# Second attention: 32 array rows per head for the transposed scores only

## The chip, the cores and the metric

One core of one Trainium2 chip runs the kernel. The time is device microseconds of one execution; three runs of the kernel before gave 1461.8, 1468.85 and 1471.88 us, and their median, 1468.85 us, is the time before.

## The reference

Two transformer layers on 2048 tokens of width 128, in float32, each modulated by vectors of a conditioning input. The first has a spectral attention (a real FFT of chunks of 64 tokens, attention on the four lowest frequencies, a causal convolution on the others) and a gated feed-forward of width 512. The second has plain attention and a mixture of eight experts, of which the two best are used. The change lies in the attention of the second layer. The core of what it must compute:

```python
qkv = (jnp.einsum('bnd,ed->bne', x, qkv_w) + qkv_b).reshape(b, n, H, 3 * HD)   # H = 16, HD = 8, n = 2048
q, k, v = jnp.split(qkv, 3, axis=-1)
...
attn = jax.nn.softmax(jnp.einsum('bhqd,bhkd->bhqk', q, k) * SCALE, axis=-1)
out = jnp.einsum('bhqk,bhkd->bhqd', attn, v)
```

## The kernel before

Five engine programs are written out by hand, and semaphores alone set the order between them. On TensorE the program is one list: what is written first runs first.

**Heads in strips.** The 16 heads form four groups (hg) of four heads (g). Head g of a group owns the 32 partitions 32g to 32g + 31. Of these, 24 hold the eight numbers of q or k three times, as parts of a split into a coarse and a fine half, so that one matmul in the reduced float format (F32R) gives products of almost full precision. Partitions 24 and 25 of the strip carry the negated maximum of each query on the side of the queries, and ones on the side of the keys. Ks holds the keys and Qs the queries of all 2048 tokens in this layout, Qp a padded copy of 512 queries: for each head a full 128-partition tile in which only that head's strip is not zero. GpSimd zeroes Qp once (L306) and refills the strips for each block of queries (L315). With all 128 rows in a matmul, the zeros of Qp keep the other three heads out of the sum.

**Two kinds of scores.** Natural scores (nat, L778) have queries on the output's partitions and serve only to find each query's maximum over the keys: 128 queries of one head against 2048 keys, four matmuls of 512 keys into PSUM banks 0 to 3. VectorE reduces two banks at a time (maxima, L1221). Transposed scores (L841) have keys on the partitions: one key tile of 128 keys (kt) against 512 queries of one head, with the maximum already subtracted by the two extra rows, into banks 4, 5 and 7 in turn (score_bank). ScalarE takes their exp into probs (L495). The values (L817) multiply probs by V; head g writes the 16 partitions from 32g of bank 6, and each is a full-precision matmul that the hardware does in two passes.

**The steps.** There are four blocks of 512 queries (qb), four groups, 16 key tiles: 256 steps (step, L821). A step s issues, in this order: L841 for heads 0 and 1; the last of the four natural matmuls of the item 20 steps ahead minus one (LEAD = 20); the four value matmuls of the step before (L808); L841 for heads 2 and 3; the first three natural matmuls of the item 20 steps ahead. The last 20 steps have no natural scores left to do. At key tile 2 four transposes of the outputs of the group before are added (turn_outputs, L805), at key tile 13 four transposes of the maxima of the next group (max_rows, L791). The chain of waits counts a step from L841 of heads 2 and 3.

**The waits.** L841 needs its bank free, that is the exp of two or three scores earlier (L835). L778 needs the maxima of its two banks (L777). L817 needs the exps of its step (L815). The first L841 of a group waits until the maxima of the group are in Qp (L825): VectorE copies them out of PSUM (L1245) and SyncE sends them in eight transfers (L277).

**Neighbouring work of other shapes.** Three other matmuls use few array rows: the mask of the first attention (L618, 32 rows, bf16, directly before L620 with 128), and two small ones of the experts (L949 and L961, 8 rows).

Of the kernel before, what the change touches and what calls it, by code (L numbers as in the profile page):

```python
# [19 lines left out]
P = 128  # L20
# [49 lines left out]
def adaln_pair(nc, x_in, consts_in, mods_in, spectral_in, ffn_in, attn_in, moe_in, out):  # L70
    with ExitStack() as ctx:
        def sb(name, shape, dt=F32, where=ctx):
            return where.enter_context(nc.sbuf_tensor(name, shape, dt))
# [78 lines left out]
        with l1:  # L152
            Ks = sb("Ks", [P, HG, TOK], F32R, where=l1)
            Qs = sb("Qs", [P, HG, TOK], F32R, where=l1)
            Qp = sb("Qp", [P, HG, G4, 512], F32R, where=l1)
# [47 lines left out]
        def bank(n):  # L203
            return ps[:, n, :]
# [8 lines left out]
        def due(count):  # L213

            return not isinstance(count, int) or count > 0
# [8 lines left out]
        score_bank, order = [], [4, 5, 7]  # L224
# [6 lines left out]
        def items_since(n):  # L231

            return next(d for d in range(1, 64) if score_bank[(n - d) % 64] == score_bank[n])
# [333 lines left out]
        def _(pe):  # L567
# [79 lines left out]
            for ri in range(2):  # L647
                pe.wait_ge(sem.gelu_ready, ri + 1)
                for half in range(2):
                    n = 2 * ri + half  # L650
# [115 lines left out]
            def nat(qb, k, c):  # L766

                hg, qt, g = k // 16 % 4, k % 16 // 4, k % 4
                item = 64 * qb + k
                if c == 0 and k % 16 == 0:  # L770
                    if isinstance(qb, int) and qb == 0 and k == 0:
                        pe.wait_ge(sem.first_filled, G4)
                    else:
                        pe.wait_ge(sem.qpad_filled, 4 * (4 * qb + k // 16))
                if c % 2 == 0:
                    if due(2 * item + c // 2 - 1):
                        pe.wait_ge(sem.nat_max, 2 * item + c // 2 - 1)  # L777
                mm = pe.matmul(bank(c), Qp[:, hg, g, qt * P:qt * P + P], Ks[:, hg, c * 512:c * 512 + 512],  # L778
                               start=True, stop=True)
                if c % 2:  # L780
                    mm.then_inc(sem.nat_ready, 1)

            def max_rows(qb, grp):

                pe.wait_ge(sem.m_step, 4 * (4 * qb + grp + 1))
                if due(4 * qb + grp):
                    pe.wait_ge(sem.o_norm, 4 * qb + grp)

                    pe.wait_ge(sem.exp_done, 256 * qb + 64 * (grp - 1) + last_in_bank_7(rows_kt) + 1)
                for qt in range(4):  # L790
                    last = pe.transpose(ps[0:8, 7, qt * P:qt * P + P], m2[:, qt, :], ident)  # L791
                last.then_inc(sem.mT_ready, 1)

            def turn_outputs(qb, grp):

                pe.wait_ge(sem.u_copied, 4 * qb + grp)
                pe.wait_ge(sem.o_norm, 4 * qb + grp)
                pe.wait_ge(sem.mT_copied, 4 * qb + grp + 1 if not (isinstance(qb, int) and 4 * qb + grp == 16) else 16)

                if isinstance(qb, int) and 4 * qb + grp == 16:  # L800
                    pe.wait_ge(sem.exp_done, 1024)
                else:
                    pe.wait_ge(sem.exp_done, 256 * qb + 64 * grp + last_in_bank_7(turn_kt) + 1)
                for qt in range(4):
                    last = pe.transpose(ps[:, 7, qt * P:qt * P + P], U[:, qt * P:qt * P + P], ident)  # L805
                last.then_inc(sem.uT_ready, 1)

            def values(qb, s):  # L808

                hg, kt = s // 16 % 4, s % 16  # L810
                if kt == 0:
                    if due(4 * qb + s // 16):
                        pe.wait_ge(sem.u_copied, 4 * qb + s // 16)
                for g in range(G4):
                    pe.wait_ge(sem.exp_done, 256 * qb + 4 * s + g + 1)  # L815
                    col = (4 * hg + g) * VW
                    last = pe.matmul(ps[32 * g:32 * g + VW, 6, :], V[:, kt, col:col + VW],  # L817
                                     probs[:, 4 * (s % 2) + g, :], start=(kt == 0), stop=(kt == 15))
                last.then_inc(sem.pv_ready, 1)

            def step(qb, s):  # L821
                hg, kt = s // 16 % 4, s % 16
                last_block = isinstance(qb, int) and qb == TB - 1
                if kt == 0:
                    pe.wait_ge(sem.mrow_in, 128 * (4 * qb + s // 16 + 1))  # L825
                for g in range(G4):

                    if g == 2 and not (isinstance(qb, int) and qb == 0 and s == 0):
                        if not (last_block and s - 1 + LEAD >= 64):
                            nat(qb, s - 1 + LEAD, 3)  # L830
                        values(qb, s - 1)
                    n = 4 * kt + g
                    free = 256 * qb + 4 * s + g - items_since(n) + 1
                    if due(free):
                        pe.wait_ge(sem.exp_done, free)  # L835
                    if n > 4 * turn_kt + 6 and n == min(m for m in range(4 * turn_kt + 7, 64) if score_bank[m] == 7):
                        pe.wait_ge(sem.o_norm, 4 * qb + s // 16 + 1)
                    if n > 4 * rows_kt + 6 and n == min(m for m in range(4 * rows_kt + 7, 64) if score_bank[m] == 7) \
                            and not (last_block and s // 16 == 3):
                        pe.wait_ge(sem.mT_copied, 4 * qb + s // 16 + 2)  # L840
                    pe.matmul(bank(score_bank[n]), Ks[:, hg, kt * P:kt * P + P], Qp[:, hg, g, :],  # L841
                              start=True, stop=True).then_inc(sem.st_ready, 1)
                if not (last_block and s + LEAD >= 64):
                    for c in range(3):
                        nat(qb, s + LEAD, c)
                if kt == turn_kt and not (isinstance(qb, int) and qb == 0 and s < 16):
                    turn_outputs(qb, s // 16)
                if kt == rows_kt and not (last_block and s // 16 == 3):
                    max_rows(qb, s // 16 + 1)
# [20 lines left out]
            for s in range(4):  # L870
                step(0, s)
            with pe.Fori(0, TB - 1) as qb:
                for s in range(4, 68):
                    step(qb, s)
            for s in range(4, 64):
                step(TB - 1, s)
# [605 lines left out]
```

## Time and profile before

| | |
|---|---|
| median of three runs | 1468.85 us (1461.8 to 1471.88) |
| profiled execution, span from first to last instruction | 1474.4 us |
| instructions | 19927 |
| mean granted TensorE clock | 0.960 |
| TensorE busy | 1334.6 us, 91% |
| TensorE weight loads busy | 798.2 us, 54% |
| VectorE busy | 879.9 us, 60% |
| ScalarE busy | 816.9 us, 55% |
| GpSimd busy | 52.3 us, 4% |

The span is the profiled execution's own time, and the only one given for it; the runs were timed apart from it. PE is a matmul, PEld a weight load; the two overlap. A matmul's duration goes from its start to the landing of its last result, so neighbours overlap too: the distance between two starts is what one costs. A matmul with many neighbours of its own shape is recorded with its weight load already done; where the load is not hidden, it is inside the recorded duration. Shapes are written rows*columns of the array.

### The profile page before, as it was taken

The page shows a single profiled execution, that of the slowest core. Times are in us where ns is not written, and L with a number is a line of the kernel's source. Part 1 is how long each engine was busy: PE and PEld are TensorE (multiplying, and loading weights), DVE is VectorE, ACT ScalarE, POOL GpSimd, SP SyncE. Part 2 cuts the span into 40 slices and gives each one's busy share as a digit, 9 for nine tenths or more (in the row PEclk, how much of TensorE's full clock was granted, in tenths as well). Part 3 has the DMA queues.
Part 4 walks back from the last instruction along what each step waited for, and adds up shares of the span by engine and source line. Part 5 has one row for each costly group of instructions (what it writes and reads, how often), then busy time and mean ns, then how long its engine had stood idle before and what let it go on. Part 6 is the DMA issues. An engine that isn't in the chain of part 4 may idle for free.

```text
span 1474.4 us, 19927 instructions
## 1 busy us (share of the span) xinstructions
PE 1334.6 (91%) x6846; PEld 798.2 (54%) x6846; DVE 879.9 (60%) x1244; ACT 816.9 (55%) x1426; POOL 52.3 (4%) x71
## 2 busy tenths in 40 slices
PE   5776999588999998999999999999999969999998
PEld 4434788334454453554444455445443337787877
DVE  4756442698877785787776777778774052222222
ACT  2425443342666675667665667667666754344342
POOL 0001000110000000000000000000000000000000
PEclk9867999899999999999998999999999989999999
DMA  8000000000000000000000000000000000000000
GB/s 334 1 1 0 0 0 1 0 0 1 1 1 2 1 1 3 2 1 1 2 2 2 2 2 1 1 2 1 1 2 1 1 0 1 8 1 8 0 7 7
DMA packets 9280, 14.83 MB, mean 10 GB/s; under 512 B 4320, under 2 KB 8544, under 8 KB 8672
## 3 DMA queue, kind: packets, MB, share of 16 engines
q1 hardware_dynamic: 8896, 10.84, 2.1%
q10 hardware_dynamic: 288, 2.76, 0.5%
q8 instruction: 53, 0.87, 0.3%
q14 instruction: 43, 0.35, 0.1%
HBM read 12.29 MB, written 1.05 MB: 9 GB/s over the span
## 4 chain that ended last, share of the span: by engine, by line
PE 75%; DVE 11%; ACT 5%; SPq 4%; DMA 3%; issue 2%; DVEq 0%; ACTq 0%
PE ps L841 18%; PE ps L817 15%; PE ps L778 13%; PE ps L941 8%; PE ps L687 5%; SPq L277 4%; PE ps L689 4%; PE ps L688 4%; DVE mx L1221 3%; DMA Qp<-mT 2%; ACT eh L547 2%; PE ps L724 1%; PE ps L922 1%; DMA x<-x_in 1%; ACT probs L495 1%
## 5 line engine op out<-in xcount | busy, mean ns | idle before, releaser
L1221 DVE TENSOR_REDUCE mx<-ps 128x1 f32<-128x1024 f32 x512 | 608.2, 1219 | 187.4 <-PE ps L778 185.4
L495 ACT ACTIVATE probs<-ps 128x512 f32<-128x512 f32 x1024 | 554.2, 595 | 277.7 <-PE ps L841 262.6
L841 PE MATMUL ps<-Qp,Ks 128*128 128x512 f32 x1024 | 356.9, 430 | 34.1 <-DMA Qp<-mT 23.1
L778 PE MATMUL ps<-Ks,Qp 128*128 128x512 f32 x1024 | 330.4, 404 | 15.4 <-DVE mx L1221 8.3
L841 PEld LDWEIGHTS ps<-Qp,Ks 128*128 128x128 f32 x1024 | 171.3, 191 | 290.0 <-ACT probs L495 226.2
L817 PE MATMUL ps<-probs,V 128*16 128x512 f32 x2048 | 275.5, 607 | 0.0
L778 PEld LDWEIGHTS ps<-Ks,Qp 128*128 128x128 f32 x1024 | 192.3, 191 | 85.8 <-DVE mx L1221 34.3
L547 ACT ACTIVATE eh<-ps,MW 128x512 f32<-128x512 f32 x128 | 88.0, 688 | 95.3 <-PE ps L689 94.6
L941 PEld LDWEIGHTS ps<-MW,eh 128*128 128x128 f32 x1024 | 118.3, 192 | 2.6
L941 PE MATMUL ps<-MW,eh 128*128 128x128 f32 x1024 | 119.2, 275 | 0.0
L1362 DVE SCALAR_TENSOR_TENSOR acc<-ps,gate,acc 128x128 f32<-128x128 f32 x128 | 36.0, 344 | 129.3 <-PE ps L941 128.8
L817 PEld LDWEIGHTS ps<-probs,V 128*16 128x16 f32 x2048 | 34.3, 94 | 91.4 <-ACT probs L495 65.3
L315 POOL CAST Qp<-Qs 32x512 fp32r (+1 forms) x60 | 36.6, 610 | 678.8 <-PE ps L841 648.8
L687 PE MATMUL ps<-hT,ew 128*128 (+1 forms) x128 | 56.7, 443 | 2.8
L689 PE MATMUL ps<-hT,ew 128*128 (+1 forms) x128 | 50.4, 394 | 0.0
L688 PE MATMUL ps<-hT,ew 128*128 (+1 forms) x128 | 50.4, 393 | 0.0
L1176 DVE TENSOR_TENSOR act_b<-bf,act_b 128x512 fp32r<-128x512 f32 x16 | 11.1, 692 | 58.9 <-ACT bf L442 58.9
L687 PEld LDWEIGHTS ps<-hT,ew 128*128 128x128 f32 x128 | 24.0, 188 | 26.7 <-ACT eh L547 21.6
L1252 DVE RECIPROCAL rden<-ps 128x16 f32<-128x16 f32 x16 | 4.0, 249 | 53.0 <-PE ps L805 53.0
L753 PE MATMUL ps<-hT,AW 128*128 128x512 f32 x64 | 32.7, 608 | 0.9 <-ACT hT L344 0.9
L677 PE MATMUL ps<-CW,z 128*128 128x128 f32 x48 | 11.7, 409 | 21.9 <-DVE z L993 21.9
L689 PEld LDWEIGHTS ps<-hT,ew 128*128 128x128 f32 x128 | 24.1, 188 | 5.7
(215 smaller groups left out, 1049.6 us busy)
## 6 DMA issues: line engine op xcount, KB each, us to landing
MW<-moe_in SPq DMA_DIRECT2D x1, 4454.0 KB, 23.7
FW<-ffn_in SPq DMA_DIRECT2D x1, 2824.5 KB, 12.4
Qp<-mT SPq DMA_DIRECT2D x128, 2.0 KB, 1.7
SW<-spectral_in ACTq DMA_DIRECT2D x1, 1479.5 KB, 9.8
DW<-mods_in ACTq DMA_DIRECT2D x1, 1219.0 KB, 6.4
x<-x_in SPq DMA_DIRECT2D x4, 256.0 KB, 10.8
out<-x SPq DMA_DIRECT2D x4, 256.0 KB, 2.3
AW<-attn_in SPq DMA_DIRECT2D x1, 836.5 KB, 13.7
```

Source lines behind the costliest of these rows:

```text
L277: sp.dma_start(Qp[row:row + 1, hg, g, :].bitcast(F32), mT[4 * part + g:4 * part + g + 1, :].bitcast(F32)) \
L315: pool.tensor_copy(Qp[rows, hg, g, :], Qs[rows, hg, cols(qb, 512)]) \
L495: act.activation(probs[:, 4 * (s % 2) + g, :], bank(score_bank[4 * (s % 16) + g]), ACT.Exp, scale=SCALE1) \
L547: act.activation(eh[:, e % 2, fb, :], bank(fb % 2), ACT.Relu, bias=mw["eb1"][:, col:col + 1]).then_inc(sem.eh_copied, 1)
L687: pe.matmul(to, w[0], v[0], start=start, stop=False)
L688: pe.matmul(to, w[0], v[1], start=False, stop=False)
L689: return pe.matmul(to, w[1], v[0], start=False, stop=stop)
L778: mm = pe.matmul(bank(c), Qp[:, hg, g, qt * P:qt * P + P], Ks[:, hg, c * 512:c * 512 + 512], start=True, stop=True)
L817: last = pe.matmul(ps[32 * g:32 * g + VW, 6, :], V[:, kt, col:col + VW], probs[:, 4 * (s % 2) + g, :], start=(kt == 0), stop=(kt == 15))
L841: pe.matmul(bank(score_bank[n]), Ks[:, hg, kt * P:kt * P + P], Qp[:, hg, g, :], start=True, stop=True).then_inc(sem.st_ready, 1)
L941: last = pe.matmul(ps[:, 2 + e % 2, qt * P:qt * P + P], eh[:, e % 2, fb, qt * P:qt * P + P], mw["ew2"][:, col:col + P], start=(fb == 0), s ...
L1221: dve.tensor_reduce(mx[:, k // 16 % 2, k % 16, pair:pair + 1], ps[:, 2 * pair:2 * pair + 2, :].rearrange("p b n -> p (b n)"), AX, ALU.max) \
```

## The change

In step, the transposed scores slice both operands to the 32 partitions of their head. The natural scores still use 128 partitions and the padded queries, and everything else is as before.

```diff
@@ -838,7 +838,8 @@
                     if n > 4 * rows_kt + 6 and n == min(m for m in range(4 * rows_kt + 7, 64) if score_bank[m] == 7) \
                             and not (last_block and s // 16 == 3):
                         pe.wait_ge(sem.mT_copied, 4 * qb + s // 16 + 2)
-                    pe.matmul(bank(score_bank[n]), Ks[:, hg, kt * P:kt * P + P], Qp[:, hg, g, :],
+                    rows = slice(32 * g, 32 * g + 32)
+                    pe.matmul(bank(score_bank[n]), Ks[rows, hg, kt * P:kt * P + P], Qp[rows, hg, g, :],
                               start=True, stop=True).then_inc(sem.st_ready, 1)
                 if not (last_block and s + LEAD >= 64):
                     for c in range(3):
```

## Rows read from the trace of the kernel before

**Rows 1.** The page: TensorE's busy time, and its granted clock in 40 slices.
```profile
PE 1334.6 (91%) x6846; PEld 798.2 (54%) x6846; DVE 879.9 (60%) x1244; ACT 816.9 (55%) x1426; POOL 52.3 (4%) x71
PEclk9867999899999999999998999999999989999999
```
**Rows 2.** Stretches of time: us, busy time of each engine, clock, DMA.
```profile
562.00:774.00 212.00, 202.08 (x1060) 102.33 (x1056) 158.38 (x157) 141.05 (x260) 9.76 (x16) 0.98 0.01 2
...
1127.00:1181.00 54.00, 47.70 (x239) 16.55 (x232) 1.23 (x3) 39.47 (x77) 0.00 (x0) 0.97 0.01 1
```
**Rows 3.** The page's costliest groups: busy us, mean ns of one, idle before.
```profile
L841 PE MATMUL ps<-Qp,Ks 128*128 128x512 f32 x1024 | 356.9, 430 | 34.1 <-DMA Qp<-mT 23.1
L778 PE MATMUL ps<-Ks,Qp 128*128 128x512 f32 x1024 | 330.4, 404 | 15.4 <-DVE mx L1221 8.3
...
L817 PE MATMUL ps<-probs,V 128*16 128x512 f32 x2048 | 275.5, 607 | 0.0
```
**Rows 4.** Chain of waits, one step: start us, us, what.
```profile
700.68 0.66 PE ps L841 x2
701.34 0.70 PE ps L778 x3
702.03 0.46 PE ps L841 x2
702.49 0.23 PE ps L778
702.72 0.98 PE ps L817 x8
```
**Rows 5.** Timeline, ScalarE and VectorE in that step: start, us, what [idle before].
```profile
701.14 2.24 ACT L495 ACTIVATE probs<-ps 128x512 f32<-128x512 f32 x4 [0.78 <-PE ps L841]
...
701.84 2.36 DVE L1221 TENSOR_REDUCE mx<-ps 128x1 f32<-128x1024 f32 x2 [0.66 <-PE ps L778]
```
**Rows 6.** Timeline of TensorE around L949, a matmul of 8 rows.
```profile
1224.73 0.39 PE L689 MATMUL ps<-hT,ew 128*128 128x512 f32 x1
1225.05 1.05 PE L949 MATMUL ps<-CW,scT 8*128 8x8 f32 x8
1226.04 0.50 PE L687 MATMUL ps<-hT,ew 128*128 128x512 f32 x1
```
**Rows 7.** Timeline of weight loads around L618, a matmul of 32 rows.
```profile
45.10 0.97 PEld L620 LDWEIGHTS ps<-Kp,QT 128*128 128x128 f32 x8 [0.23 <-issue]
46.19 0.09 PEld L618 LDWEIGHTS ps<-mcol,mrow 32*128 32x128 bf16 x1
46.51 0.30 PEld L620 LDWEIGHTS ps<-Kp,QT 128*128 128x128 f32 x2 [0.23 <-issue]
```
**Rows 8.** Timeline of loads and matmuls: a pair L841, and the first of L817.
```profile
700.61 0.30 PEld L841 LDWEIGHTS ps<-Qp,Ks 128*128 128x128 f32 x2 [0.85 <-ACT probs L495]
...
702.64 0.12 PEld L817 LDWEIGHTS ps<-probs,V 128*16 128x16 f32 x6 [0.35 <-ACT probs L495]
...
702.64 0.62 PE L817 MATMUL ps<-probs,V 128*16 128x512 f32 x4
```
**Rows 9.** Chain of waits in the last 20 steps.
```profile
1150.83 0.61 ACT probs L495
...
1151.47 0.49 PE ps L841
```
**Rows 10.** Timeline of TensorE around a group's end.
```profile
716.19 0.73 PE L841 MATMUL ps<-Qp,Ks 128*128 128x512 f32 x2
...
718.89 0.72 PE L841 MATMUL ps<-Qp,Ks 128*128 128x512 f32 x2 [1.27 <-DMA Qp<-mT]
...
720.76 0.73 PE L841 MATMUL ps<-Qp,Ks 128*128 128x512 f32 x2
```
**Rows 11.** Chain of waits ahead of that matmul, one issue and the last transfer.
```profile
713.28 0.59 SPq L277
...
717.07 1.70 DMA Qp<-mT
```

## The prediction

> **What bounds the kernel now.** First the page: TensorE is busy 91% of the span and its granted clock is 0.9 to 1.0 of full speed where the second attention runs [rows 1]. The stretches by time place that attention: about 355 to 1181 us, in four blocks of queries; over 562 to 774 us TensorE is busy 202 of 212 us, VectorE 158, ScalarE 141 [rows 2]. So TensorE sets the pace, if the others really wait for it. The groups say which work this is: 1024 transposed scores (L841), 1024 natural ones (L778), 2048 half passes of the values (L817), 963 us of matmul together [rows 3].
>
> Then one step (one key tile of four heads) in the chain of waits: two L841 take 0.66 us, three L778 0.70, two L841 0.46, one L778 0.23, eight L817 0.98, ending at 703.70, 3.02 us after the step's start [rows 4]. The chain never leaves TensorE. The other engines confirm it: ScalarE's four exps take 2.24 us and begin after 0.78 us of waiting for L841, VectorE's two maxima take 2.36 us after 0.66 us of waiting for L778 [rows 5]. A shorter TensorE step would shorten the kernel by up to about 0.6 us a step before VectorE binds; a longer one lengthens it at once.
>
> The reader should see one more thing: the same two matmuls cost 0.66 us behind L817 and 0.46 behind L778 [rows 4]. This 0.20 is what the rest turns on.
>
> **The change, part by part.** It adds and removes no instruction. L841 reads 32 rows of the array instead of 128. That has two effects.
>
> First, a change of array shape between neighbours. Matmuls of 128 rows, 128 columns and 512 elements follow each other by 0.23 us (three in 0.70 [rows 4]), and the next weights are loaded under the running one. L689 begins at 1224.73; the next, L949, has 8 rows, and begins 0.32 later; going back, L687 at 1226.04 lasts 0.50 instead of 0.39 to 0.40, because its weight load (0.11 us of array time) stands in the open [rows 6]. So one switch costs (0.32 - 0.23) + (0.50 - 0.39) = 0.20 us, the same as the difference in the chain. Is it the rows, or a semaphore? L618 (32 rows) to L620 (128 rows) has no wait between: L618's weights at 46.19, L620's at 46.51; and from L620 to L618, 46.19 follows on eight loads that ended at 46.07, instead of beginning under the last matmul [rows 7]. Both directions pay without a semaphore in play. I take 0.195 a switch; from these rows it can hardly be under 0.19 or over 0.20.
>
> A step has two switches today, L778 to L817 and L817 to L841. After the change it has five: L817 to L841 and L778 to L817 remain, and L841 to L778, L778 to L841, L841 to L778 are new. Three times 0.195 is 0.585 us a step.
>
> Second, the two L841 that stand side by side now lie in different strips of 32 rows and write different PSUM banks. No row here shows two row strips at work together, so their gain is bounded. One end is nothing: today's pairs take their 0.23 us each in turn. The other end is the nearest relative, L817, where four matmuls in four strips of columns, 0.60 us each, fit in 0.62 us, and their weight loads (six in 0.12 us) overlap too [rows 8]. By that a pair costs one matmul plus about 0.01, a gain of 0.22; two pairs give 0.44 a step. Between them: matmuls overlap but weight loads don't. The pair's loads take 0.30 us today [rows 8] and one has 0.11 of array time, so the second starts 0.11 behind the first, and a pair gains 0.12, two 0.24. I take 0.44, since L817 is the same array cut the other way.
> The Trainium skill states this directly ("TensorE: Matmul & The Clock Gate", Part 3, The mechanism: weight loads overlap only where row groups differ, and tiles start about 4 ns apart). By it the gain is the one that I took; no run here shows it for rows yet.
>
> A step so becomes 3.02 + 0.585 - 0.44 = 3.165 us, 0.145 longer.
>
> How many steps: L778's 1024 matmuls are 256 items, of which 20 are done ahead of the first step, so 236 steps have natural scores. The last 20 have none. There the chain goes L841, exp 0.61, L841 0.49, values, over and over [rows 9]: their switches exist already, and the two L841 around the exp can't be paired, because the second waits for the exp of the first. No gain, no loss.
>
> Where a stall gives back: at a group's end TensorE waits for the eight transfers of the maxima. The step that starts at 716.19 takes 4.57 us, 1.55 more than others, and the matmul waits 1.27 us for the DMA [rows 10]. From the copy of the maxima to the landing nothing depends on TensorE: eight issues of 0.59 us one after the other and 1.70 of transfer [rows 11]. Two steps run under it, so twice the lengthening is absorbed as long as that is under 1.5 us: 0.29 at each of the 14 group ends among the 236 steps. That is as if 28 of the steps cost nothing: 208 x 0.145 = 30 us.
>
> What I cost at nothing: VectorE and ScalarE do the same work with longer waits. The exp of the third head must end before the weights of the next step's second L841 can load; today that wait doesn't show: two L841 behind L778 keep their 0.46 [rows 4], and a new switch puts 0.2 us more ahead of that load. POOL's fill of the padded queries, the zeroed tile and the transfers stay as they are. If the cover failed, up to 0.2 us at a few steps would be exposed, some us in all.
>
> **Sum:** the profiled span is 1474.4 us; no device time of that execution stands beside it, and it lies 5.5 us over the median of the runs, 1468.85. The difference is added to the median: 1468.85 + 30 = 1499 us.
>
> **Rivals.**
> A. Weight loads of the two strips come one after the other: 0.585 - 0.24 = 0.345 a step, 0.69 absorbed at group ends, 208 x 0.345 = 72 us, 1541 us. For it: today's loads stand 0.11 apart. Against it: L817's overlap.
> B. No overlap at all between row strips: 0.585 a step, still under the 1.5 absorbed, 122 us, 1591 us. For it: no row shows it for rows. Against it: the columns do it.
> C. Faster. The place is the three new switches; the price that decides is 0.44 / 3 = 0.147 us. If the weight load across a switch were hidden for strips (a load into rows that the running matmul doesn't use) only 0.09 of each would remain: 3 x 0.09 - 0.44 = -0.17 a step, 208 x -0.17 = -35 us, 1434 us, with VectorE's 2.36 still inside a step of 2.85. Against it: L618 and L689 to L949 pay in full though one side has few rows.
> D. Nothing happens: the slice doesn't make the array smaller, or price and gain cancel within the measurement. The slices of 32 and 8 rows elsewhere do show as 32 and 8 rows with a switch [rows 6, 7], so only the cancelling is left: a switch of about 0.15 to 0.17.
> A fall of the granted clock is no case of its own: in the last 20 steps TensorE waits for ScalarE every step and was granted 0.97 [rows 2].
>
> **How the numbers follow.** My forecast has a chance of 0.60; its own range is 1489 to 1510 (switch 0.185 to 0.205, pair gain 0.21 to 0.23, some us for a stall that shifts). A 0.17, B 0.06, C 0.08, D 0.09. Below 1484 and above 1545 lie C, most of D and B, about 0.2 in all. A measurement tells 1% (15 us) from no change: slower 0.83, same 0.09, faster 0.08.
>
> **What would show it.** L841 with 32 rows; steps of about 3.17 us; in the chain, three L778 taking 0.89 instead of 0.70 and the single one 0.43; weight loads of a pair a few ns apart (A: 0.11 apart, B: matmuls 0.23 apart); each new weight load starting about 0.32 us after the start of the last matmul; group ends with a DMA wait of about 1.0 us. I am wrong if L778's weights load under L841 across the switch, if a pair doesn't overlap, or if the granted clock falls inside the blocks.

## The result: 6.5% slower, and the profile after

The changed kernel takes 1568.21 us (median of four runs, 1553.31 to 1581.53) against 1468.64 (the kernel before, a fourth run added): ratio 1.0648, 95% interval 1.0581 to 1.0715. Medians here are of all runs, ratios of each kernel's fast runs alone (here without the 1581.53). Forecast were 1499 us and a range up to 1545. The sign was right and the size was not: about 100 us instead of 30.

The steps themselves came out as forecast. The chain of waits of the changed kernel, one step at full clock (start us, us, what), answers to [rows 4]:

```profile
701.62 0.42 PE ps L842 x2
702.05 0.89 PE ps L778 x3
702.94 0.43 PE ps L842 x2
703.38 0.42 PE ps L778
703.80 0.98 PE ps L817 x8
704.78 0.43 PE ps L842 x2
```

L842 is the old L841. The step takes 3.16 us (704.78 - 701.62; forecast 3.165, before 3.02). A pair behind L817 costs 0.42 where it cost 0.66. Three L778 cost 0.89 where they cost 0.70, the single one 0.42 where it cost 0.23: the new switches. The timeline of the same step shows the overlap (PE is a matmul, PEld a weight load):

```profile
701.55 0.18 PEld L842 LDWEIGHTS ps<-Qp,Ks 32*128 32x128 f32 x2 [0.85 <-ACT probs L495]
...
701.55 0.49 PE L842 MATMUL ps<-Qp,Ks 32*128 32x512 f32 x2
```

The pair's loads take 0.18 us for both, against 0.30 in [rows 8], and its matmuls 0.49 for both: two row strips work side by side, as the four column strips of L817 do. The Trainium skill's figure for this ("TensorE: Matmul & The Clock Gate", Part 3, The mechanism: tiles start about 4 ns apart) is confirmed to the rounding of the rows.

Then the same chain 60 us earlier:

```profile
643.96 0.72 PE ps L842 x2
644.68 1.58 PE ps L778 x3
...
646.98 0.72 PE ps L778
647.70 1.84 PE ps L817 x8
649.54 0.72 PE ps L842
```

The same work, but 5.58 us (649.54 - 643.96). Every piece is stretched, and nothing waits for another engine. The stretches of time tell why (start and end, length, busy time of PE, PEld, DVE, ACT and POOL with the number of instructions, and behind POOL the granted clock):

```profile
531.00:553.00 22.00, 22.00 (x68) 8.20 (x68) 9.15 (x11) 8.95 (x17) 0.00 (x0) 0.50 0.00 1
...
597.00:655.00 58.00, 54.81 (x168) 18.52 (x164) 25.14 (x23) 22.31 (x41) 0.00 (x0) 0.56 0.01 2
...
915.00:1215.00 300.00, 293.71 (x1509) 110.64 (x1507) 222.86 (x222) 201.06 (x372) 7.29 (x12) 1.00 0.01 1
...
1229.00:1278.00 49.00, 40.40 (x171) 9.74 (x170) 0.55 (x2) 27.96 (x54) 0.00 (x0) 0.64 0.00 0
```

TensorE was granted 0.50, its level of 1.2 GHz ("half clock" below), for long stretches. The slices of the page show them against [rows 1]:

```profile
PE 1431.1 (91%) x6846; PEld 725.3 (46%) x6846; DVE 882.0 (56%) x1244; ACT 817.0 (52%) x1426; POOL 52.1 (3%) x71
PEclk9768998995999796599998889999999678999999
```

TensorE is 91% busy in both kernels, so the busy share says nothing here. The mean granted clock does: 0.906 against 0.960. With only two levels, a mean clock c over a span S means 2(1 - c)S at the lower one: 295 us against 118. The expectations below count half-clock time so. A good part of it is not the change's: in both kernels some 80 us lie ahead of the first step and 14 to 19 behind the last. Inside the steps the traces have 199 us against 24.

The account of the 97 us between the profiled spans (1571.5 and 1474.4), from the distances between one step's values (L817) and the next one's in both traces:

- The first step's values begin 2 us later.
- 198 of the first 235 distances ran at full clock in both kernels. Group ends included, they add 25 us.
- The other 37 ran at half clock at least in part, in one kernel or in both. They add 57 us.
- The last 20 steps add 14 us. Ten of them took 4.03 us or more, where most had taken 2.63.

Together 98 us; behind the steps half a microsecond comes back. The steps' own 0.147 us is also in the 37, some 5 us. So the price of the steps is 30 us, as forecast, and the clock's is about 67, most of it in some 24 steps at 5.58 instead of 3.17. In the last 20 steps the chain reads:

```profile
1225.19 1.84 PE ps L817 x8
1227.03 0.77 PE ps L842 x3
1227.80 0.60 ACT probs L495
1228.44 0.79 PE ps L842
1229.23 1.84 PE ps L817 x8
```

Here 128 rows had run at 0.97 of the full clock [rows 2, second row], also with a wait for an exp in each step.

### The profile page after: what moved, and what is told of

Its sections match the earlier page's. It is cut to its first block, busy times and chain, and to the rows that moved or that the text cites. A ratio compares the mean times of both kernels' runs of the same rounds, so it can differ in the third digit from the quotient of the medians.

```text
span 1571.5 us, 19927 instructions
## 1 busy us (share of the span) xinstructions
PE 1431.1 (91%) x6846; PEld 725.3 (46%) x6846; DVE 882.0 (56%) x1244; ACT 817.0 (52%) x1426; POOL 52.1 (3%) x71
## 4 chain that ended last, share of the span: by engine, by line
PE 76%; DVE 10%; ACT 5%; SPq 4%; DMA 2%; issue 2%; DVEq 0%; ACTq 0%
PE ps L778 19%; PE ps L817 16%; PE ps L842 14%; PE ps L942 7%; PE ps L687 5%; SPq L277 4%; PE ps L689 4%; PE ps L688 4%; DVE mx L1222 3%; DMA Qp<-mT 2%; ACT eh L547 1%; PE ps L724 1%; PE ps L923 1%; ACT probs L495 1%; DMA x<-x_in 1%
## 5 line engine op out<-in xcount | busy, mean ns | idle before, releaser
L778 PE MATMUL ps<-Ks,Qp 128*128 128x512 f32 x1024 | 407.7, 482 | 14.6 <-DVE mx L1222 7.4
L842 PE MATMUL ps<-Qp,Ks 32*128 32x512 f32 x1024 | 279.4, 537 | 36.2 <-DMA Qp<-mT 18.0
L817 PE MATMUL ps<-probs,V 128*16 128x512 f32 x2048 | 304.6, 668 | 0.0
L842 PEld LDWEIGHTS ps<-Qp,Ks 32*128 32x128 f32 x1024 | 104.1, 196 | 385.0 <-ACT probs L495 301.6
L778 PEld LDWEIGHTS ps<-Ks,Qp 128*128 128x128 f32 x1024 | 185.1, 203 | 178.2 <-issue 92.4
L817 PEld LDWEIGHTS ps<-probs,V 128*16 128x16 f32 x2048 | 34.6, 96 | 71.1 <-issue 55.7
L753 PE MATMUL ps<-hT,AW 128*128 128x512 f32 x64 | 32.7, 608 | 0.9 <-ACT hT L344 0.9
```

The lines of the kernel that those rows point to most:

```text
L842: pe.matmul(bank(score_bank[n]), Ks[rows, hg, kt * P:kt * P + P], Qp[rows, hg, g, :], start=True, stop=True).then_inc(sem.st_ready, 1)
```

## The experiments

Medians are in us; ratios are to the kernel before, with 95% intervals; two experiments have none. Half-clock times are those of the one profiled execution of each kernel. An idle matmul is one whose result is overwritten; the expectations call such matmuls fill.

### Prices of switch and overlap

**64 rows** for the transposed scores: the same switches, no overlap.
```diff
-                    rows = slice(32 * g, 32 * g + 32)
+                    rows = slice(64 * (g // 2), 64 * (g // 2) + 64)
```


> The transposed scores read 64 rows (the half of the array in which the head lies; the padded queries are zero in the other head's strip), so each step has the three new switches of array shape, but two neighbours share their rows and can't overlap. Theory of the prices (switch 0.195 us, overlap of a pair 0.22 us): full-clock step 3.02 + 0.585 = 3.60 us, against 3.17 in the changed kernel. On the clock: the changed kernel's record shows 296 us at half clock against 121 before. If the open gaps at the switches keep the clock down after a stall, this kernel has the same gaps and shows long slow stretches too (over 200 us at half clock, time 1600 to 1680 us). If it is the small number of rows or the overlap of the pairs that does it, the slow stretches shrink (under 160 us, time about 1590 us).

Measured: 1725 (1691 to 1783), mean clock of the profiled run 0.869, so 454 us at half clock. A full-clock step in its chain:

```profile
499.80 0.89 PE ps L778 x3
500.69 0.66 PE ps L842 x2
501.35 0.42 PE ps L778
501.78 0.98 PE ps L817 x8
502.76 0.66 PE ps L842 x2
```

With 0.66 for the pair, 3.61 us: the price of the switch holds, and without overlap a pair costs 0.23 more. The time is above both branches of the expectation. The slow stretches are longer than in the changed kernel (346 us at half clock inside the steps, against 199), for example:

```profile
620.00:820.00 200.00, 197.66 (x499) 70.67 (x501) 77.30 (x73) 67.39 (x124) 4.86 (x8) 0.50 0.00 1
```

They are there without any overlap, so overlap isn't needed for them.

**Heads 2 and 3 only**, and **heads 0 and 1 only**:
```diff
-                    rows = slice(32 * g, 32 * g + 32)
+                    rows = slice(32 * g, 32 * g + 32) if g > 1 else slice(0, 128)    # the other kernel: if g < 2
```


> Only the transposed scores of heads 2 and 3 read 32 rows, those of heads 0 and 1 keep 128. Behind the values a switch stands anyway, so only one switch is new (L842 to L778) and one pair overlaps: 3.02 + 0.195 - 0.22 = 2.995 us a step by the theory of the prices, some 5 us less than before in all, 1460 to 1470 us if the clock behaves as before. If overlap and few rows harm the clock in proportion, half-clock time lies between 121 and 296 us and the time between 1475 and 1510.

> Only heads 0 and 1 read 32 rows: two new switches and one overlapping pair, 3.02 + 0.39 - 0.22 = 3.19 us a step by the theory of the prices, about 35 us over the kernel before at its clock (1500 us); more than that is the clock. If the clock goes by switch gaps, its half-clock time is above that of the kernel with heads 2 and 3; if it goes by overlap or rows alone, the two have the same.

Measured: heads 2 and 3, 1473.7, ratio 1.0021 [0.9985, 1.0056]; heads 0 and 1, 1512.2, ratio 1.0281 [1.0247, 1.0316]. Chains of the first and of the second:

```profile
672.26 0.43 PE ps L842
...
675.26 0.42 PE ps L842
```
```profile
670.56 0.66 PE ps L842 x2
...
673.76 0.66 PE ps L842 x2
```

Steps of 3.00 and 3.20 us, 2.995 and 3.19 forecast. Only the pair beside L817 (heads 2 and 3) pays for its switch, and just so. The times lie 4 us above the forecast range and 12 us above the forecast. Their mean clocks, 0.958 and 0.956, are close to that of the kernel before (0.960): with half of the transposed scores on 32 rows the clock held. Inside the steps they spent 25 and 35 us at half clock, the kernel before 24.

### Rows or gaps?

**All scores on 32 rows**: L778 is sliced like L842. No new switch is left.
```diff
-                mm = pe.matmul(bank(c), Qp[:, hg, g, qt * P:qt * P + P], Ks[:, hg, c * 512:c * 512 + 512],
+                rows = slice(32 * g, 32 * g + 32)
+                mm = pe.matmul(bank(c), Qp[rows, hg, g, qt * P:qt * P + P], Ks[rows, hg, c * 512:c * 512 + 512],
```


> The natural scores read 32 rows per head too, so no switch of shape is left between the two kinds of scores, and all their neighbours in different strips can overlap. Theory of the prices: at most 3.02 - 0.44 = 2.58 us a step, down to VectorE's 2.36; 1330 to 1380 us. On the clock: if few rows in use keep the clock down after a stall, half-clock time stays well above 200 us here and takes back a good part of the gain (1400 us or more); if the switch gaps do it, half-clock time is near the 121 us of the kernel before.

Measured: 1781, ratio 1.2115 [1.2011, 1.222]: the fastest step so far and the slowest kernel, far above the 1330 to 1380 of the first branch. Two stretches of it:

```profile
450.00:735.00 285.00, 283.42 (x1042) 103.70 (x1043) 159.89 (x154) 137.97 (x256) 7.30 (x12) 0.50 0.01 1
760.00:790.00 30.00, 27.62 (x163) 10.52 (x163) 25.70 (x26) 21.18 (x41) 2.20 (x4) 1.00 0.01 2
```

At full clock a step takes 2.59 to 2.83 us, 2.68 on average; at half clock 4.27, and every fourth 4.46. TensorE stays at half clock for these 285 us, in which it is busy all but 1.6. No gap explains that. The Trainium skill ("TensorE: Matmul & The Clock Gate", Part 1) says that sustained matmul work releases the throttle; here sustained work did not, with all scores on 32 rows and the values (128 rows, 16 columns) between them, and the measurement decides.

**Only the natural scores on 32 rows** (the kernel before, with the edit above):

> The opposite choice: natural scores on 32 rows, transposed ones on 128. Three new switches a step as with 64 rows for the transposed scores, and no overlap (the natural matmuls side by side all lie in one strip), so 3.60 us a step at full clock by the price of the switch. Fewer rows in use than with 64 rows (1725 us, 457 us at half clock). If the clock goes by rows in use, half-clock time and the time are higher than there (over 1750 us); if it goes by the gaps at the switches, they are the same.

Measured: 1637, ratio 1.109 [1.1021, 1.1158]. This refutes what I had expected of it. The steps have the same length at full clock as with 64 rows (3.62), fewer rows are in use in sum, and yet inside the steps the slow stretches are short, 41 us in all:

```profile
648.00:672.00 24.00, 21.10 (x68) 8.02 (x68) 9.89 (x11) 8.68 (x16) 0.00 (x0) 0.66 0.01 3
672.00:1320.00 648.00, 637.29 (x2840) 245.89 (x2832) 425.31 (x410) 381.34 (x705) 19.42 (x32) 0.98 0.01 1
```

So the gaps at the switches are not enough to cause the long stretches: this kernel has as many as the one with 64 rows. Its mean clock was 0.925 to 0.944 in four runs, that of the other 0.837 to 0.895.

Most of its half clock lies ahead of the steps, which begin 47 us late. The same stretch there, first of the kernel before, then of this one, and a part of this one's timeline:

```profile
283.00:389.00 106.00, 94.57 (x338) 48.26 (x339) 93.67 (x102) 46.15 (x73) 7.32 (x12) 0.95 0.00 1
```
```profile
283.00:389.00 106.00, 105.44 (x150) 39.47 (x150) 61.97 (x66) 22.68 (x29) 7.28 (x12) 0.50 0.00 0
```
```profile
330.53 2.08 PE L753 MATMUL ps<-hT,AW 128*128 128x512 f32 x2
332.54 1.22 PE L779 MATMUL ps<-Ks,Qp 32*128 32x512 f32 x2
333.69 2.08 PE L753 MATMUL ps<-hT,AW 128*128 128x512 f32 x2
```

In both kernels the stretch begins at half clock, at the end of the same wait of 4.42 us for ScalarE. With 128 rows the full clock is back after 3.4 us. With 32 rows it stays away for 106 us, although TensorE is busy for all but half a microsecond of them, and although 2.0 of each 3.15 us go to matmuls of 128 rows (L753 and L762, which make keys, queries and values). The two scores of a pair lie in one strip here and don't overlap. The kernel with all scores on 32 rows has half clock there too, for 72 us. So the natural scores on 32 rows do keep the clock down in this place, and hardly in the steps. A plain sum of rows in use is not the rule.

### What throws the clock, and what brings it back

**The loop over query blocks written out** on TensorE, so that its jump goes away (the kernel before is idle for 3.5 us there, once in a block), **five idle matmuls at group ends**, and **both**:
```diff
                 if kt == 0:
+                    if not (isinstance(qb, int) and qb == 0 and s == 0):
+                        pe.wait_ge(sem.exp_done, 256 * qb + 4 * s - items_since(0) + 1)
+                        for _ in range(5):
+                            pe.matmul(bank(score_bank[0]), Ks[:, hg, 0:P], Ks[:, hg, 0:512], start=True, stop=True)
                     pe.wait_ge(sem.mrow_in, 128 * (4 * qb + s // 16 + 1))
...
-            with pe.Fori(0, TB - 1) as qb:
+            for qb in range(TB - 1):
                 for s in range(4, 68):
                     step(qb, s)
```


> The changed kernel with TensorE's loop over the blocks of queries written out, so that its sequencer doesn't stand still at a jump (3.9 us before the third key tile of a block). In the changed kernel the slow stretches (steps of 5.59 us instead of 3.17) begin at the stage's start, at a block's end and behind the jump. If such stalls only pull the clock down and the few rows keep it down, fewer stretches begin: half-clock time 150 to 250 us, 1510 to 1550 us. If the stretches come of themselves, without a stall, nothing but the jumps' 12 us goes away: 1555.

> The changed kernel with five idle matmuls of 128 rows (their result is overwritten) while TensorE waits for the maxima at a group's end, so about 1.15 of the 1.2 us of waiting is filled. If the waits at group ends pull the clock down, half-clock time falls well below 296 us; if only the jumps do it, it stays near that and so does the time, 1560 us. The fill itself costs nothing at full clock, at half clock about 1 us each time.

> Both together. If the price beyond the 30 us of the steps is the clock after stalls, this comes to about 1468 + 30 - 12 (jumps) = 1485 us with half-clock time near 121 us. If the price lies elsewhere, it stays over 1540.

Measured: 1514.4, ratio 1.0304 [1.0233, 1.0376]; 1537.8, ratio 1.0405 [1.0326, 1.0484]; 1517.0, ratio 1.0323 [1.0288, 1.0358]. With both, no slow step is left between the first three and the last 13; the kernel still misses the 1485 that I gave it, by the half clock at the two ends of the stage, and by idle matmuls that outlast the wait (group ends take 4.86 us instead of 4.36). The loop written out does as much alone: its trace has two slow spots of 3 and 10 us between, each at a group end. The slow stretches in the blocks do begin at stalls.

**The same idle matmuls and loop in the kernel before**, and **128 rows again in the last 20 steps** of the changed one:
```diff
-                    rows = slice(32 * g, 32 * g + 32)
+                    rows = slice(0, 128) if last_block and s + LEAD >= 64 else slice(32 * g, 32 * g + 32)
```


> The kernel before with the same fill and the same loop written out, as a measure of what these two alone do: the jumps' 12 us away, some us for fill that outlasts the wait, 1455 to 1465 us. The difference between this kernel and the one with 32 rows for the transposed scores is then what the change costs with the clock held: 30 to 40 us.

> Fill at group ends and loop written out as before, and in the last 20 steps the transposed scores keep 128 rows. Measured with 32 rows there: 12 of those steps at 4.03 us, with 128 rows in the kernel before 2.64. If rows in use are what the clock goes by, these steps run at 2.64 again and the time falls by about 16 us from 1517 to about 1500; if the clock falls there because TensorE waits for exps, it stays at 1517.

Measured: 1456.8, ratio 0.9891 [0.9862, 0.992], and 1505.4, ratio 1.022 [1.0188, 1.0252]. The last steps of the changed kernel with both (idle matmuls and loop written out), first with 32 rows, then with 128:

```profile
1165.00:1223.00 58.00, 48.14 (x189) 10.98 (x189) 0.55 (x2) 32.13 (x63) 0.00 (x0) 0.58 0.00 1
```
```profile
1173.00:1222.00 49.00, 42.86 (x210) 15.31 (x208) 1.70 (x5) 36.52 (x70) 0.00 (x0) 1.00 0.00 1
```

With all but the stage's first steps at full clock, the change costs 1505 - 1457 = 48 us, more than the 30 to 40 expected: some 30 for the steps and most of the rest at the stage's start, where this profile shows five steps at 5.59.

**Only the last 20 steps on 32 rows, or on 64**, in the kernel before with the idle matmuls at group ends and the written-out loop. No switch is new there and ScalarE sets the step's length:
```diff
+                    rows = slice(32 * g, 32 * g + 32) if last_block and s + LEAD >= 64 else slice(0, 128)
-                    pe.matmul(bank(score_bank[n]), Ks[:, hg, kt * P:kt * P + P], Qp[:, hg, g, :],
+                    pe.matmul(bank(score_bank[n]), Ks[rows, hg, kt * P:kt * P + P], Qp[rows, hg, g, :],
```


> The kernel before with fill and loop written out (1457 us), and only in its last 20 steps the transposed scores on 32 rows. There is no natural matmul there, so no switch is new, and the wait for the exps sets the pace, so the step is 2.63 us either way. Measured with 32 rows there, after steps of the changed kernel: 12 steps of 4.03 us. If the rows alone make TensorE fall to half clock and stay, some 10 steps of 4.03 appear again: 1470 to 1475 us. If it needs the changed steps ahead of it, nothing happens: 1457.

> The same with 64 rows, so that two neighbours of one half can't overlap. If the overlap is what matters, no step of 4.03 us appears (1457 us); if the rows do, some appear (1460 to 1475).

Measured: 32 rows 1480.3, ratio 1.005 [1.0017, 1.0083], 23 us above the same kernel with 128 rows; 64 rows 1464.8, ratio 0.9966 [0.9936, 0.9997], 8 us above it. The last steps with 32, with 64 and with 128 rows:

```profile
1139.00:1180.00 41.00, 34.20 (x131) 7.24 (x123) 0.00 (x0) 21.28 (x42) 0.00 (x0) 0.52 0.00 0
```
```profile
1139.00:1173.00 34.00, 26.94 (x143) 9.33 (x142) 1.87 (x5) 24.11 (x46) 0.00 (x0) 1.00 0.00 0
```
```profile
1124.00:1175.00 51.00, 44.82 (x227) 16.78 (x220) 2.15 (x6) 37.26 (x72) 0.00 (x0) 1.00 0.00 1
```

The steps ahead are untouched and no switch is added. With 32 rows the clock falls at 1117 us for 14 us, is back after the five idle matmuls of the group's end, and falls again at 1141 us up to the stage's end. The step then takes 4.03 us, so ScalarE no longer sets it. The mean clocks of the ten runs, 0.946 to 0.961, all lie below those of the same kernel with 128 rows (0.969 to 0.975, four runs). With 64 rows the profiled run shows only one fall, of 3 us; the mean clocks of its ten runs, 0.940 to 0.973 and mostly under 0.969, say that the clock fell more in others, which fits the 8 us.

The rows are not all that changes, though. At full clock the timelines of a step read, with 32 and with 128 rows:

```profile
1134.09 0.52 PE L846 MATMUL ps<-Qp,Ks 32*128 32x512 f32 x3
1135.27 0.50 PE L846 MATMUL ps<-Qp,Ks 32*128 32x512 f32 x1 [0.66 <-ACT probs L495]
```
```profile
1127.16 0.96 PE L845 MATMUL ps<-Qp,Ks 128*128 128x512 f32 x3
1128.35 0.50 PE L845 MATMUL ps<-Qp,Ks 128*128 128x512 f32 x1 [0.23 <-ACT probs L495]
```

Three scores in three strips run at once, so TensorE waits 0.66 us for the exp instead of 0.23 (0.45 with 64 rows). This pair therefore doesn't tell fewer rows from longer waits. That half clock can last almost without waits is shown by the two stretches above in which TensorE was busy nearly all the time.

### A version that uses all this

**All scores on 32 rows with seven idle matmuls of 128 rows at group ends, the loop written out.**

> All scores on 32 rows, with seven idle full-row matmuls at group ends and the loop written out. Measured without these: 2.63 us a step at full clock, 4.27 at half clock, and half clock for 1123 us. If a stall alone throws it into half clock and at full clock it stays there, this comes to about 1468 - 208 x 0.39 - 12 = 1375 us. If 32 rows can't hold the full clock at all, it stays near 1750.

Measured: 1510.8, ratio 1.0262 [1.021, 1.0313], 270 us below the same kernel without these two, and between the 1375 and the 1750 of the expectation. Its chain at the end of the first group (L829 are the idle matmuls) shows the clock come back:

```profile
454.31 3.29 PE ps L829 x7
457.59 0.72 PE ps L847
458.32 1.88 PE ps L818 x8
...
464.73 0.98 PE ps L818 x8
```

The idle matmuls ran at half clock themselves (3.29 us), and a few us after them L818 takes 0.98 instead of 1.88. In this profile that happened at each of the five group ends that the kernel reached at half clock, and the stretches that had lasted 285 us and more now ended within a group.

**Full rows in the last 20 steps and in the natural scores ahead of the first step, and five idle matmuls ahead of the transposed maxima**, then with **16 idle matmuls ahead of the first step** and two, or none, ahead of the maxima:
```diff
             pe.wait_ge(sem.o_norm, 1)
+            for _ in range(16):
+                pe.matmul(bank(score_bank[0]), Ks[:, 0, 0:P], Ks[:, 0, 0:512], start=True, stop=True)
             for s in range(4):
                 step(0, s)
```


> All scores of the steps on 32 rows, with idle full-row matmuls at group ends (seven) and ahead of the transposed maxima (five), the loop written out, and 128 rows in the last 20 steps and for the natural scores ahead of the first step, where other engines set the pace. If full rows keep the clock and a stall is what throws it: 208 steps at 2.65 instead of 3.02, 1375 to 1400 us, faster than the kernel before by 5%. If 32 rows lose the clock in spite of it, about 1450 to 1500.

> The fastest variant so far (all scores of the steps on 32 rows; 1465 us median, 1440 in the profile) lost 30 us at half clock in its first 18 steps and 15 times 1.3 us to five idle matmuls that outlasted the wait ahead of the transposed maxima. Here 16 idle full-row matmuls stand ahead of the first step and two instead of five ahead of the maxima. If full rows bring the clock back: 1390 to 1410 us. If it then falls at key tile 13 again: 1420 to 1450.

> The same with no idle matmuls ahead of the transposed maxima: 1385 to 1400 us if the clock holds there, 1420 to 1460 if that wait throws it, as it did in 4 of 15 groups of the variant without them.

Measured: 1465.0 (1441.8 to 1490.0); 1456.5, ratio 0.9885 [0.9848, 0.9922]; 1439.9, ratio 0.9823 [0.975, 0.9896]. The last beats the kernel before by 1.0 to 2.5% and the changed one by 8%. None reaches its better branch: the first and the last lie in their worse one, the second above both of its own. The clock still falls in some groups and stays down to the next group end, where the seven idle matmuls brought it back each time; five ahead of the maxima, in the first of the three, had not (they ran at 407 us, the clock came back at 426). The last one's worst stretch, and the one after it:

```profile
735.00:812.00 77.00, 75.49 (x308) 29.18 (x309) 44.36 (x43) 38.35 (x72) 3.74 (x7) 0.61 0.01 2
812.00:1132.00 320.00, 305.81 (x1779) 117.14 (x1777) 227.22 (x227) 232.87 (x446) 7.28 (x12) 1.00 0.01 1
```

## Why the prediction was wrong

**What bounds the kernel**: right. TensorE sets the step, in all variants at full clock, until VectorE or ScalarE take over near 2.6 to 2.7 us (I had named 2.36, VectorE's two maxima alone).

**The price of a switch**, 0.195 us: right. The steps with one, two and three new ones came out at 3.00, 3.20 and 3.16 to 3.61 us. Reading it from L618 and L949 [rows 6, 7], far from the change, was enough.

**The overlap of a pair**, 0.22 us: right, and L817 was the right neighbour to take it from. Rivals A and B fall with the loads of a pair taking 0.18 us for both; C and D fall with the switch's full price. That the measured 1568 us lie between A's 1541 and B's 1591 is chance.

**The number of steps and the absorbed waits**: right in kind. At full clock the group end's step went from 4.57 to 4.36 us, and its DMA wait from 1.27 [rows 10] to 1.02 us:

```profile
729.75 0.60 PE L842 MATMUL ps<-Qp,Ks 32*128 32x512 f32 x2 [1.02 <-DMA Qp<-mT]
```

**The last 20 steps**: "No gain, no loss" held at full clock, because the exps set the step. That nothing can be paired there did not: three scores run at once, and TensorE waits longer for the exp.

**The step that failed** is the sentence "A fall of the granted clock is no case of its own: in the last 20 steps TensorE waits for ScalarE every step and was granted 0.97 [rows 2]." It drew from matmuls of 128 rows what matmuls of 32 rows would do, and put the clock at nothing in the sum. In those same 20 steps the changed kernel was granted 0.64, and it spent 199 us of its steps at half clock instead of 24. The term that was left out is the larger one: some 67 of the 97 us. The prediction did name a fall of the clock inside the blocks as a sign of being wrong, but gave it neither a price nor a chance.

What is shown: the lost time is time at half clock. In the blocks the falls begin at stalls: at block and group ends, at the loop's jump, at the stage's start. With 128 rows the clock is back after 3 to 7 us. With the transposed scores on 32 rows it often stays down for 10 to 44 us, on 64 rows for up to 208, and with all scores on 32 rows for up to 382. Half clock can last while TensorE hardly waits at all. Seven idle matmuls of 128 rows in a row brought the full clock back each time.

What stays open: what the chip counts. A count of rows doesn't fit: 64 rows did more harm in the blocks than 32, and less in the last 20 steps; the natural scores on 32 rows harmed the clock ahead of the steps and little inside them. In the last 20 steps fewer rows and longer waits come together and no run separates them. Where a slow stretch ends by itself is also not explained.

## What to carry to other kernels

Slicing a padded matmul to its own rows is worth its overlap (0.22 us a pair here) only where no 128-row matmul stands between: each switch of array shape costs 0.195 us. Before counting such a gain, read the granted clock of every stage and ask what happens after each stall if the matmuls that follow use fewer rows; a kernel of 2.68 us steps was 21% slower than one of 3.02. If few rows are wanted, first remove the stalls (the written-out loop gave back 54 us alone), then fill the waits that are left with idle 128-row matmuls, and check that these end before the wait does.

## What the runs showed of the hardware that I had not expected

TensorE busy for 283 of 285 us, with all scores on 32 rows, was granted 0.50 all the while, and 1.00 from 25 us later on, on the same work. The state that it is in persists: the same steps ran steadily at either level. Seven matmuls in a row of 128 rows and 512 elements (3.29 us) were followed by the full clock each time, but 128-row matmuls in two thirds of the time, in turn with scores of 32 rows, were not in 106 us. Three scores in three row strips took 0.52 us together where three of 128 rows took 0.96. Writing the loop out and filling the group ends gained 1.1% in the kernel before as well (ratio 0.9891).
